# Layer 3 feed-forward: SyncE issues the gate and up load of the next tile before the down load of this one

## The reference, cut to what matters

```python
x = hidden_states.reshape(n_tokens, h)            # 512 tokens, 512 features
perm = jnp.argsort(flat_expert)                   # pairs (token, expert), sorted by expert
gate = ragged_dot(x[tok], gate_weight.T, group_sizes)
up = ragged_dot(x[tok], up_weight.T, group_sizes)
h_act = jax.nn.silu(gate) * up
down = ragged_dot(h_act, down_weight.T, group_sizes)
out = zeros.at[tok].add(down * w_sorted[:, None])
```

## Time and profile before

| what | value |
|---|---|
| median of 3 runs | 2156.8 us |
| time of the profiled execution | 2163.69 us |
| its span, first instruction to last | 2161.5 us |
| mean granted clock of TensorE over the span | 0.964 |
| TensorE busy over the span | 1973.5 us, 91% |
| DMA queue q1 (SyncE's loads) | 163.90 MB, 22.5% of 16 engines |
| DMA queue q0 (GpSimd's) | 23.10 MB, 5.6% of 16 engines |

### The profile page before, as it was taken

One profiled execution on the slowest core, in us unless ns is written; L12 is line 12 of the kernel. 1 busy time (PEld: TensorE's weight loads), 2 busy tenths in 40 slices (PEclk: granted clock), 3 DMA queues, 4 the chain that ended last, 5 costly groups with the idle time before them and its releaser, 6 DMA issues.

```text
span 2161.5 us, 38438 instructions
## 1 busy us (share of the span) xinstructions
PE 1973.5 (91%) x14580; PEld 1560.8 (72%) x14580; DVE 1061.3 (49%) x2477; ACT 889.4 (41%) x1819; POOL 567.5 (26%) x416
## 2 busy tenths in 40 slices
PE   6989999996997999986899999999999999798886
PEld 6977777885446878774587777999989999633333
DVE  5546666764114366688747777333234555410111
ACT  4346666532223455566655544422253232211110
POOL 3333332322342211000031110333241110145553
PEclk9999999998998999997999999999999999899998
DMA  3200010238355221141020000222220000468895
GB/s 125 77 25 29 14 42 5 70 126 310 71 88 126 76 83 55 66 157 44 5 72 34 29 15 3 89 62 58 68 77 24 29 28 2 169 193 258 264 279 154
DMA packets 67918, 189.22 MB, mean 88 GB/s; under 512 B 15114, under 2 KB 16366, under 8 KB 62510
## 3 DMA queue, kind: packets, MB, share of 16 engines
q1 hardware_dynamic: 50606, 163.90, 22.5%
q0 software_dynamic: 17152, 23.10, 5.6%
HBM read 224.56 MB, written 20.91 MB: 114 GB/s over the span
## 4 chain that ended last, share of the span: by engine, by line
PE 75%; DVE 8%; DMA 7%; ACT 4%; issue 3%; SPq 1%; POOL 1%; ACTq 0%; DVEq 0%; POOLq 0%
PE psum L106 16%; PE psum L109 15%; PE psum L107 15%; DMA l3f_weights<-in_l3f_gate_up_dram 4%; PE psum L1580 4%; PE psum L900 3%; PE psum L3610 3%; PE psum L3578 2%; PE psum L2801 2%; PE psum L3596 2%; PE psum L1607 2%; PE psum L926 2%; PE psum L2447 1%; PE psum L3032 1%; PE psum L139 1%
## 5 line engine op out<-in xcount | busy, mean ns | idle before, releaser
L1580 PE MATMUL psum<-l3f_weights,l3f_x_turned 128*64 (+1 forms) x768 | 131.0, 498 | 30.6 <-issue 16.6
L1580 PEld LDWEIGHTS psum<-l3f_weights,l3f_x_turned 128*64 128x64 f32 x768 | 58.1, 148 | 94.2 <-issue 72.3
L2238 ACT ACTIVATE l2x_probs<-psum,l2x_shift 100x361 f32<-100x361 f32 x128 | 70.2, 562 | 97.3 <-DVE l2x_shift L2293 97.3
L1875 POOL TENSOR_TENSOR l2x_ctx_lo<-l2x_ctx_raw,l2x_ctx_hi 128x1448 fp32r<-128x1448 f32 x8 | 26.4, 3297 | 314.9 <-ACT l2x_ctx_hi L1883 314.9
L1676 DVE TENSOR_TENSOR l3f_h<-l3f_silu,psum 128x352 f32<-128x352 f32 x24 | 12.5, 522 | 164.4 <-ACT l3f_silu L1662 156.0
L3749 ACT ACTIVATE l0x_probs<-l0x_probs,l0x_lowest 100x361 f32<-100x361 f32 x128 | 75.2, 588 | 42.1 <-DVE l0x_lowest L3918 42.1
L106 PE MATMUL psum<-xn_hi,l2f_w_gu_hi 128*128 128x400 f32 x256 | 88.6, 346 | 1.6 <-DVE xn_lo L192 1.3
L448 POOL TENSOR_TENSOR l2f_w_gu_lo<-l2f_raw_gu,l2f_w_gu_hi 128x512 fp32r<-128x512 f32 x32 | 43.0, 1357 | 174.2 <-ACT l2f_w_gu_hi L463 174.2
L107 PE MATMUL psum<-xn_lo,l2f_w_gu_hi 128*128 128x400 f32 x256 | 87.8, 343 | 0.0
L2476 ACT ACTIVATE ln_squares<-l1x_clipped,l1x_key_shift,l1x_key_scale 128x400 f32<-128x400 f32 (+1 forms) x96 | 62.3, 712 | 51.4 <-DVE l1x_clipped L2515 51.4
L3918 DVE CUSTOM_DVE_ANT_0 l0x_probs<-psum,l0x_outside 100x361 f32<-100x361 f32 x128 | 62.9, 531 | 32.1 <-PE psum L3578 29.6
(11 more groups left out here) (553 smaller groups left out, 6120.9 us busy)
## 6 DMA issues: line engine op xcount, KB each, us to landing
l3f_weights<-in_l3f_gate_up_dram SPq DMA_DIRECT2D x24, 1408.0 KB
l3f_weights<-in_l3f_down_dram SPq DMA_DIRECT2D x24, 768.0 KB
l0x_w_raw<-in_slabs_dram SPq DMA_DIRECT2D x52, 256.0 KB, 2.6
l0f_weights<-in_slabs_dram SPq DMA_DIRECT2D x8, 1536.0 KB
l1x_piece<-in_bit_w_dram SPq DMA_DIRECT2D x8, 1024.0 KB, 6.4
l1f_raw<-in_bit_w_dram SPq DMA_DIRECT2D x8, 1024.0 KB, 8.3
l2f_raw_gu<-in_slabs_dram SPq DMA_DIRECT2D x32, 256.0 KB, 2.6
l0x_ctx_raw<-in_ctx_dram SPq DMA_DIRECT2D x8, 724.0 KB, 4.2
```

The costliest lines, as they stand in the source:

```text
L1580: mm = pe.matmul(c.psum[lanes, bank + x, 0:self.INNER], self.x_turned[:, t % 2, k, lanes], weights, start=k == 0, stop=k == KD - 1)
L1875: pool.tensor_tensor(self.ctx_lo[:, q, :, :], self.ctx_raw[:, :, :], self.ctx_hi[:, q, :, :], ALU.subtract).then_inc(self.s("ctx_split"), 1)
L2238: act.activation(self.probs[:, m % 2, g, :], c.psum[0:S, g, 0:C], ACT.Exp, bias=self.shift[:, g:g + 1], scale=self.SCALE, accum_out=self.t ...
```

## The change

load_ring is cut into three: ring_row reads the table, load_gate_up waits and issues the gate and up load, load_down waits and issues the down load. In the prefetch the order stays as it was. In the loop of sync, SyncE issues gate and up of tile 3 first, and then for each tile t from 3 on: the table row and gate and up of t + 1, and then the down load of t. The waits of each load, the places and the sizes are the same. The registers of two tiles' rows are live at a time.

```diff
--- before.py
+++ after.py
@@ -1479,13 +1479,19 @@
                            self.tile_values[:, x, :, :].rearrange("p x t -> p (x t)"), start=x == 0, stop=x == n - 1)
         mm.then_inc(c.sem("table_units"), 1)
 
-    def load_ring(self, c, sp, t):
+    def ring_row(self, sp, t):
+        return sp.value_load(self.ring_rows[0:1, t:t + 1], min_val=0, max_val=P * (self.experts - 1))
+
+    def load_gate_up(self, c, sp, t, at):
 
         q = t % self.RING
-        at = sp.value_load(self.ring_rows[0:1, t:t + 1], min_val=0, max_val=P * (self.experts - 1))
         wait(sp, self.s("gate_up_units"), t - self.RING + 2 if t >= self.RING else 0)
         sp.dma_start(self.weights[:, q, 0:self.DOWN_AT],
                      c.a["l3f_gate_up"][bass.DynSlice(at, P), :]).then_inc(self.s(f"gate_up_landed{q}"), 16)
+
+    def load_down(self, c, sp, t, at):
+
+        q = t % self.RING
         wait(sp, self.s("d_units"), t - self.RING + 2 if t >= self.RING else 0)
         sp.dma_start(self.weights[:, q, self.DOWN_AT:self.ROW],
                      c.a["l3f_down"][bass.DynSlice(at, P), :]).then_inc(self.s(f"down_landed{q}"), 16)
@@ -1508,7 +1514,9 @@
         sp.wait_ge(c.sem("tables"), 4)
         sp.dma_start(self.second_rows[:, :], self.rows[self.PART:P, :]).then_inc(self.s("second_rows"), 16)
         for t in range(self.RING):
-            self.load_ring(c, sp, t)
+            at = self.ring_row(sp, t)
+            self.load_gate_up(c, sp, t, at)
+            self.load_down(c, sp, t, at)
         for b in range(4):
             self.write_rows(c, sp, b)
 
@@ -1518,8 +1526,14 @@
             self.write_rows(c, sp, b)
         sp.dma_start(c.out[:, :, self.tokens:T], c.residual[:, :, self.tokens:T]).then_inc(c.sem("out_written"), 16)
         sp.wait_ge(self.s("x_landed0"), 16)
+        at = self.ring_row(sp, self.RING)
+        self.load_gate_up(c, sp, self.RING, at)
         for t in range(self.RING, self.TILES):
-            self.load_ring(c, sp, t)
+            this, at = at, None
+            if t + 1 < self.TILES:
+                at = self.ring_row(sp, t + 1)
+                self.load_gate_up(c, sp, t + 1, at)
+            self.load_down(c, sp, t, this)
         sp.wait_ge(self.s("d_units"), self.TILES)
         for x in range(2):
             sp.wait_ge(self.s(f"added_up{x}"), 16 * self.TILES)
```

## The result

The changed kernel takes 2178.5 us (median of 8 runs, 2167.1 to 2188.6) where the kernel before took 2156.95 us in the same comparison: a ratio of 1.009, 95% interval 1.006 to 1.012. A second set of runs gave 1.0093 (1.0068 to 1.0119). The forecast was 2131.4 us, faster. The sign was wrong.

The account below looks back on a forecast made before the run. Late loads, next GpSimd's spare loads, were taken to bound the stage: 20 x (10.59 - 9.44) = 23.0 us plus 2.4 us gives 25.4 us, 2156.8 - 25.4 = 2131.4 us; range 2116 to 2149 us.

Parts of the forecast that it names:

- What can be won, 38.3 + 2.4 us: Tiles 3 to 23: 38.3 us lost at 10.59 against 8.67 us a tile, plus 2.4 us for the slow last product.
- The gate and up load leaves some 4.5 us earlier and ends no wait any more: SyncE's queue: tile 4's load leaves at 1910.0 instead of 1914.5, lands 3 us before TensorE could start, off the chain.
- Table reads and down loads cost nothing: SyncE's queue: the 0.8 us table read runs under waits; the down load has some 10 us of cover.
- The hidden path through GpSimd's spare loads: GpSimd's queue: additions and spare loads, slowed by big loads, form a second path to the product of nearly the same length.
- L: Spare load's issue to gate and up product: 3.2 us with engines quiet, 6.3 beside big loads, middle 4.75 us taken.
- The round over two tiles: Spare-load path in the changed stage: 9.28 + 4.85 + 4.75 = 18.9 us for two tiles, 9.44 us a tile.
- The products of 6.6 us and more are gone: TensorE's gate and up products slowed after waits (6.60 to 7.84 us where others take 4.96) were to disappear.
- The rule of the Trainium skill: DMA engines alternate queues by packet; cited for the rival that spare loads stay slow, 2143 to 2151 us, chance 0.18.
- The rival "Slower": GpSimd's additions find fewer holes between big loads and land late: 11.5 us a tile, 18 us more, 2175 us; chance 0.07.
- DMA work holds the stage at 9.13 us a tile: Check on the stage: two tiles move 5.53 MB at 303 GB/s, share 0.97, 18.3 us, so 9.13 us a tile.

## Why the prediction was wrong

- *What can be won, 38.3 + 2.4 us, and that it lies in this stage*: right. The changed order without the spare loads took 2121.2 us, 38 us less than its own kernel before.
- *The gate and up load leaves some 4.5 us earlier and ends no wait any more*: right; 3.3 us ahead of the down load instead of 1.1 us behind it are 4.4 us, and no load of SyncE stands in the chain of the stage.
- *Table reads and down loads cost nothing*: right; the run at the old time with the new order took 2155.3 us, and without the spare loads TensorE waits for no down load of the ring.
- *The hidden path through GpSimd's spare loads*: right. Removing it from the kernel before alone gave 14 us, for which its 1.2 to 1.7 us ahead of every second product had stood as "issue". It was even the longer of the two: by the landings in the trace of before, the spare load of every tile from 4 to 23 lands last, 0.2 to 1.8 us behind the ring's load, so that moving the ring's load could win only as far as the spare load did not come later. Without the spare loads TensorE's waits there, 16.0 us, end on the ring's load.
- *L, from the spare load's issue to the product, 4.75 us*: this step failed. I took the middle between 3.2 and 6.3 us and took it for harmless that "the next big load goes out close to the spare load's issue". It went out 0.3 us ahead of it, and L was 6.3 us at tile 3, 10.2 at tile 7, 7.4 at tile 9 (1977.64 to 1985.01), and 7.45 us on average over the ten tiles. This is the sign that I had named for L being wrong, and it lies even beyond my upper end. Only the rows of before had been taken for its ends, and in those no big load was issued in the 3 us ahead of a spare load. Both events hang on fixed steps: the big load on the end of the gate and up product, the spare load on y, two additions and a spare down load, 4.85 us of issuing. The rows of before had both times, and I did not set them side by side: from the start of a product 9.28 + 4.85 = 14.1 us to the spare load, and 8.67 + 4.95 = 13.6 us to the end of the next product, at which the next big load leaves.
- *The round over two tiles*: right in form. From 1961.20: 11.6 us to the next addition (2.3 of them the slow product), 4.85 to the spare load, 7.4 to the product, together 23.8 us, 11.9 a tile instead of 9.44.
- *The products of 6.6 us and more are gone*: wrong, for the same reason. There are seven of them and they cost 15.4 us, a term that the sum had at nothing.
- *The rule of the Trainium skill*, that an engine takes turns between its queues a packet at a time (DMA: Bandwidth & Descriptors, "Queues, rings and completion order"): I let it speak only for a small gain, 2149 us. The trace does not show what a packet in that sense is. If a turn is as long as a whole big load's share of an engine, which would fit the 99 packets to 2, the rule speaks for a loss where a small load that is wanted soon is issued just behind a big one that is wanted late.
- *The rival "Slower"*: the size by accident. Its additions never waited for a landing.
- *DMA work holds the stage at 9.13 us a tile*: wrong by little; at 306 GB/s and a share of 0.97 the kernel with early spare loads ran at 8.87, and two of its tiles moved 306 x 17.75 = 5.43 MB, not 5.53.

Open: why a load cut in four helps the changed kernel and not the one before, and what makes the time from a spare load's first landing to its last, 0.8 to 4.6 us at the ten tiles: the big load itself, GpSimd's own earlier loads, which it had slowed, or single parts held up by something else. The additions and the gather share the queue with the spare loads, and no run took either away by itself.

## What to carry to other kernels

Before issuing a large load earlier, list the small loads of the other queues that are issued within its length behind it, and ask which of them is wanted before the large one has landed. Move those ahead first: here that was free, since their own waits had ended long before, and it turned a loss of 20 us into a gain of 33. Being issued ahead is not enough by itself: some 1 us ahead of the big load still left some of a spare load's parts late. Where the profile ends a wait in "issue" just behind a landing, look for a second wait of the same instruction; here it was the next bound.

## What the runs showed of the hardware that I had not expected

- A load that moves no row at all took 6.2 to 10.2 us from issue to use where a load of 1408 KB was issued at nearly the same time, and landed in 2.1 to 4.0 us where that load was 8.6 us or more ahead. Its first landing moved with the size of the other load: some 2 us, 3.3 to 3.4 behind 704 KB, 5.0 to 5.5 behind 1408 KB.
- Two queues on the same engines do not share them evenly: 99 packets of one against 2 of the other in 2.8 us (1911.5 to 1914.3), with loads issued to both.
- A count raised by an empty instruction behind a DMA on GpSimd went up before GpSimd had issued that DMA (SyncE left at 1910.05, GpSimd issued at 1910.37). So such a count did not tell that the DMA was on its way.
- The spread from run to run differs much: 2167.1 to 2188.6 us for the changed kernel (8 runs), 2124.5 to 2128.1 for the changed order with early spare loads (4 runs), and for the kernel before 2155.5 to 2160.3 in one comparison (8 runs) and 2149.5 to 2172.6 in another (14 runs). What sets it is not shown.
